# Ternary feed-forward stage: rounded values transposed in fp32, rounding constant removed in ScalarE's copies, silu waiting for the gate product alone

## What is computed

```python
def _weight_quant(w):                       # three matrices, 256 x 1024
    scale = 1.0 / jnp.clip(jnp.mean(jnp.abs(w)), 1e-05)
    return jnp.clip(jnp.round(w * scale), -1.0, 1.0) / scale
def _act_quant(x):                          # per token
    scale = 127.0 / jnp.clip(jnp.max(jnp.abs(x), axis=-1, keepdims=True), 1e-05)
    return jnp.clip(jnp.round(x * scale), -128.0, 127.0) / scale
def _bitlinear(x, w):
    return jnp.einsum('bsi,oi->bso', _act_quant(x), _weight_quant(w))
gate = jax.nn.silu(_bitlinear(x, w_gate))
up = _bitlinear(x, w_up)
return _bitlinear(gate * up, w_down)        # x = x + tanh(g_ffn[1]) * this
```

## Time and profile before

| | us |
|---|---|
| median of 3 runs | 3035.04 |
| lowest and highest | 3032.43, 3036.76 |
| time of the profiled execution | 3036.45 |
| its span | 3034.7 |
| busy in the span: PE, DVE, ACT, POOL | 2558.5, 1635.7, 1290.4, 1218.0 |
| the stage's part of the span | about 857 to 1099 |

### The profile page before, as it was taken

One profiled execution on the slowest core, in us unless ns is written; L12 is line 12 of the kernel. 1 busy time (PEld: TensorE's weight loads), 2 busy tenths in 40 slices (PEclk: granted clock), 3 DMA queues, 4 the chain that ended last, 5 costly groups with the idle time before them and its releaser, 6 DMA issues. The chain is left out here.

```text
span 3034.7 us, 43762 instructions
## 1 busy us (share of the span) xinstructions
PE 2558.5 (84%) x13250; PEld 1481.8 (49%) x13251; DVE 1635.7 (54%) x3292; ACT 1290.4 (43%) x2566; POOL 1218.0 (40%) x1717
## 2 busy tenths in 40 slices
PE   7997999999936647898888889779957886799997
PEld 4554667666613323334343343345534475466664
DVE  5884656555457844665647556378846534222221
ACT  4663435344335532554545446446641232222221
POOL 3665651344446631111120210036890243566663
PEclk9998999999978877999999999989988965899998
DMA  3001000001000004131221221010003241122222
GB/s 122 5 1 60 0 0 1 1 1 42 1 31 0 0 11 89 38 74 47 48 59 47 52 63 38 1 49 15 8 1 111 85 141 54 35 46 45 45 45 31
DMA packets 86053, 117.22 MB, mean 39 GB/s; under 512 B 13864, under 2 KB 64144, under 8 KB 84080
## 3 DMA queue, kind: packets, MB, share of 16 engines
q1 hardware_dynamic: 68944, 96.01, 11.0%
q0 software_dynamic: 16928, 18.93, 4.0%
HBM read 80.00 MB, written 34.64 MB: 38 GB/s over the span
## 5 line engine op out<-in xcount | busy, mean ns | idle before, releaser
L2986 ACT ACTIVATE L2S_pT<-L2S_t_ps 128x512 f32<-128x512 f32 (+3 forms) x768 | 353.7, 490 | 234.7 <-PE L2S_t_ps L2884 125.7
L3065 DVE TENSOR_REDUCE L2S_mx<-L2S_s_ps 128x1 f32<-128x768 f32 (+7 forms) x384 | 347.1, 951 | 110.0 <-PE L2S_s_ps L2863 106.3
L2881 PE MATMUL L2S_t_ps<-L2S_q,L2S_k 98*128 98x512 bf16 (+3 forms) x768 | 250.7, 340 | 41.1 <-ACT L2S_pT L2986 33.1
L2862 PE MATMUL L2S_s_ps<-L2S_k,L2S_q 96*128 96x512 bf16 (+3 forms) x768 | 207.0, 342 | 44.8 <-DVE L2S_mx L3065 33.8
L3170 POOL DMA_DIRECT2D L2S_q<-L2S_mrow x32 | 17.2, 537 | 430.1 <-DVE L2S_mrow L3073 430.1
L3524 DVE TENSOR_TENSOR L3B_h<-L3B_si,L3B_u_ps 128x512 f32<-128x512 f32 x71 | 48.8, 687 | 237.5 <-PE L3B_u_ps L3467 237.5
L571 POOL TENSOR_TENSOR L_prob<-L_prob,L_rc 128x616 f32<-128x616 f32 x64 | 77.9, 1217 | 234.7 <-DVE L_rc L524 234.7
L2881 PEld LDWEIGHTS L2S_t_ps<-L2S_q,L2S_k 98*128 98x128 bf16 x768 | 75.4, 99 | 191.4 <-ACT L2S_pT L2986 147.6
L3441 POOL DMA_INDIRECT out<-L3B_y,L3F_rows x71 | 114.7, 1616 | 132.8 <-DVE L3B_y L3530 118.3
L2899 PE MATMUL L2S_o_ps<-L2S_pT,L2S_v 128*32 128x512 f32 (+3 forms) x1536 | 166.3, 507 | 0.0
L310 PE MATMUL L_scores<-weights,L_xT 128*128 128x308 f32 x512 | 143.1, 423 | 2.2 <-ACT L_xT L426 1.6
(11 more groups left out here) (496 smaller groups left out, 5997.9 us busy)
## 6 DMA issues: line engine op xcount, KB each, us to landing
qk_parts<-L2S_part SPq DMA_DIRECT2D x96, 128.0 KB, 2.3
L2S_q<-qk_parts SPq DMA_DIRECT2D x32, 192.0 KB, 3.6
L2S_k<-qk_parts SPq DMA_DIRECT2D x32, 192.0 KB, 3.5
L2S_q<-qk_parts SPq DMA_DIRECT2D x32, 128.0 KB, 3.3
L2S_k<-qk_parts SPq DMA_DIRECT2D x32, 128.0 KB, 3.3
self_attended<-L2S_att SPq DMA_DIRECT2D x4, 1024.0 KB, 4.3
L_xn<-self_attended SPq DMA_DIRECT2D x8, 512.0 KB, 3.5
L2F_wgu<-in_L_gu SPq DMA_DIRECT2D x8, 512.0 KB, 8.0
```

The source lines that it names most:

```text
L2862: nc.tensor.matmul(o[:, z * 512 + c:z * 512 + e], lhs, k6[0:KR, q % 2, h, c:e], start=True, stop=(e < end))
L2881: mm = nc.tensor.matmul(o[:, lo:512], k6[:, q % 2, j, kt * P:(kt + 1) * P], q6[:, q % 2, j, c * 512 + lo:(c + 1) * 512], start=True, stop= ...
L2986: nc.scalar.activation(pT[:, st % 2, j, lo:512], t_ps[j % 2][:, lo:512], ACT.Exp, scale=SK).then_inc(s["exp_done"], 1)
L3065: nc.vector.tensor_reduce(dst, src, AX.X, ALU.max).then_inc(s["mx_done"], 1)
```

## The change

Eight edits in `ternary_stage`, nothing elsewhere. DVE's rounding of x ends with fp32 values that still hold ROUND (xq); L1972 is gone, and with it the cut at 127. PE transposes xq and hq themselves, in fp32, with the fp32 identity, to fp32 PSUM; hT_ps takes two banks for that, xT_ps still one, and the weights' sums go to o_ps, so that m_ps is gone. ACT's two copies subtract ROUND as they write bf16. DVE's shift and its phase are gone, and PE's turn_h waits for ACT's quantise. The semaphore gu_full is split: g_full behind the gate product, for silu; u_full behind the up product, for DVE's multiply. The gate product waits for silu of the tile before, the up product for DVE's product of the tile before. ACT's quantise of hq waits for the transposes of two tiles before, which now read that buffer. The bf16 identity is gone.

```diff
-        xT_ps, hT_ps, o_ps = ps("xT_ps", [P, 1024], BF16), ps("hT_ps", [P, INNER], BF16), ps("o_ps", [P, 512])
-        m_ps = ps("m_ps", [P, 512])
-        identb = sb("identb", [P, P], BF16)
+        xT_ps, hT_ps, o_ps = ps("xT_ps", [P, 512]), ps("hT_ps", [P, INNER]), ps("o_ps", [P, 512])
...
-                    mm = nc.tensor.transpose(xT_ps[:, k * P:(k + 1) * P], xqb[:, p, k * P:(k + 1) * P], identb[:])
+                    mm = nc.tensor.transpose(xT_ps[:, k * P:(k + 1) * P], xq[:, p, k * P:(k + 1) * P], chip.ident[:])
...
-                pe.wait_ge(s["h_done"], t + 1)
-                for o, n in ((g_ps, "gate"), (u_ps, "up")):
+                for o, n, full in ((g_ps, "gate", "g_full"), (u_ps, "up", "u_full")):
+                    pe.wait_ge(s[("silu_done", "h_done")[n == "up"]], t + 1)
...
-                mm.then_inc(s["gu_full"], 1)
+                    mm.then_inc(s[full], 1)
...
-                pe.wait_ge(s["hqb_done"], t + 3)
+                pe.wait_ge(s["hq_done"], t + 3)
...
-                    mm = nc.tensor.transpose(hT_ps[:, k * P:(k + 1) * P], hqb[:, p, k * P:(k + 1) * P], identb[:])
+                    mm = nc.tensor.transpose(hT_ps[:, k * P:(k + 1) * P], hq[:, p, k * P:(k + 1) * P], chip.ident[:])
...
-                nc.scalar.activation(xT[:, p, :, :].rearrange("p k t -> p (k t)"), xT_ps[:, 0:D], ACT.Copy).then_inc(s["xT_free"], 1)
+                nc.scalar.activation(xT[:, p, :, :].rearrange("p k t -> p (k t)"), xT_ps[:, 0:D], ACT.Copy, bias=-ROUND).then_inc(s["xT_free"], 1)
...
-                act.wait_ge(s["gu_full"], t + 1)
+                act.wait_ge(s["g_full"], t + 1)
...
-                act.wait_ge(s["hqb_done"], t + 1)
+                act.wait_ge(s["hT_full"], t + 1)
...
-                nc.scalar.activation(hT[:, p, :, :].rearrange("p k t -> p (k t)"), hT_ps[:], ACT.Copy).then_inc(s["hT_free"], 1)
+                nc.scalar.activation(hT[:, p, :, :].rearrange("p k t -> p (k t)"), hT_ps[:], ACT.Copy, bias=-ROUND).then_inc(s["hT_free"], 1)
...
-            link(nc.vector.tensor_copy(identb[:], chip.ident[:]))
...
-                link(nc.vector.tensor_scalar(xq[:, p, :], xn[:, p, :], ix[:, p:p + 1], ROUND, ALU.mult, ALU.add))
-                nc.vector.tensor_scalar(xqb[:, p, :], xq[:, p, :], ROUND + 127.0, -ROUND, ALU.min, ALU.add).then_inc(s["xq_done"], 1)
+                nc.vector.tensor_scalar(xq[:, p, :], xn[:, p, :], ix[:, p:p + 1], ROUND, ALU.mult, ALU.add).then_inc(s["xq_done"], 1)
...
-                dve.wait_ge(s["silu_done"], t + 1)
+                dve.wait_ge(s["silu_done"], t + 2)
+                dve.wait_ge(s["u_full"], t + 1)
...
-            def shift(t, q):
-                p = q % 2
-                dve.wait_ge(s["hq_done"], t + 3)
-                dve.wait_ge(s["hT_full"], t + 1)
-                nc.vector.tensor_scalar(hqb[:, p, :], hq[:, p, :], ROUND + 127.0, -ROUND, ALU.min, ALU.add).then_inc(s["hqb_done"], 1)
...
-            pipelined(dve, [stats, normalise, quantise, multiply, shift, none, none], unroll=4)
+            pipelined(dve, [stats, normalise, quantise, multiply, none, none, none], unroll=4)
```

More of the change, by code:

```diff
@@ L1814, in ternary_stage @@
         stat, mv, ve, rs = sb("stat", [P, 2, 6]), sb("mv", [P, 2, 2]), sb("ve", [P, 2]), sb("rs", [P, 2])
-        xn, xq, xqb, xT = sb("xn", [P, 2, D]), sb("xq", [P, 2, D]), sb("xqb", [P, 2, D], BF16), sb("xT", [P, 2, KD, P], BF16)
+        xn, xq, xT = sb("xn", [P, 2, D]), sb("xq", [P, 2, D]), sb("xT", [P, 2, KD, P], BF16)
         am, ax, ix = sb("am", [P, 2]), sb("ax", [P, 4]), sb("ix", [P, 2])
         gs, us = sb("gs", [P, 4]), sb("us", [P, 4])
-        h, hq, hqb, hT = sb("h", [P, 2, INNER]), sb("hq", [P, 2, INNER]), sb("hqb", [P, 2, INNER], BF16), sb("hT", [P, 2, IK, P], BF16)
+        h, hq, hT = sb("h", [P, 2, INNER]), sb("hq", [P, 2, INNER]), sb("hT", [P, 2, IK, P], BF16)
         ah, ai, s2, ev = sb("ah", [P, 2]), sb("ai", [P, 2]), sb("s2", [P, 2]), sb("ev", [P, 4])
         minus1, res = sb("minus1", [P, 1]), sb("res", [P, 2, D])
-        names = """pre abs_done mean_done tern_done stats_done rstd_done xn_done ix_done xq_done xT_full xT_free gu_full silu_done
-            h_done ah_done s2_done hq_done hqb_done hT_full hT_free o_full o_free x_done dve_step pool_step act_step wmean_done""".split()
+        names = """pre abs_done mean_done tern_done stats_done rstd_done xn_done ix_done xq_done xT_full xT_free g_full u_full silu_done
+            h_done ah_done s2_done hq_done hT_full hT_free o_full o_free x_done dve_step pool_step act_step wmean_done""".split()
         s = {n: sem(n) for n in names}
@@ L1836, in _ @@
             pe.wait_ge(s["abs_done"], 3)
-            nc.tensor.matmul(m_ps[:, 0:3], chip.ones[:], rowsum[:], start=True, stop=True).then_inc(s["mean_done"], 1)
+            nc.tensor.matmul(o_ps[:, 0:3], chip.ones[:], rowsum[:], start=True, stop=True).then_inc(s["mean_done"], 1)
             pe.wait_ge(s["tern_done"], 4)
@@ L1883, in _ @@
             act.sem_inc(s["hq_done"], 2)
+            act.sem_inc(s["silu_done"], 1)
             for n, name in enumerate(order):
@@ L1927, in _ @@
         def _(dve):
-            link = Links(dve, s["dve_step"], [1, 1, 1, 1, 0, 0, 0])
+            link = Links(dve, s["dve_step"], [1, 1, 0, 1, 0, 0, 0])
             link.k = 0
-            link(nc.vector.tensor_copy(identb[:], chip.ident[:]))
             dve.wait_ge(s["mean_done"], 1)
-            link(nc.vector.tensor_scalar(wmean[:], m_ps[:, 0:3], 1.0 / COUNT, 1e-5, ALU.mult, ALU.max))
+            link(nc.vector.tensor_scalar(wmean[:], o_ps[:, 0:3], 1.0 / COUNT, 1e-5, ALU.mult, ALU.max))
             nc.vector.reciprocal(wscale[:], wmean[:]).then_inc(s["wmean_done"], 1)
@@ L1944, in _ @@
             dve.sem_inc(s["h_done"], 1)
-            dve.sem_inc(s["hqb_done"], 2)
             link.start = link.k
@@ L1965, in quantise @@
                 p = q % 2
-                link.enter(2, t)
                 dve.wait_ge(s["ix_done"], t + 3)
                 dve.wait_ge(s["xT_full"], t + 1)
-                link(nc.vector.tensor_scalar(xq[:, p, :], xn[:, p, :], ix[:, p:p + 1], ROUND, ALU.mult, ALU.add))
-                nc.vector.tensor_scalar(xqb[:, p, :], xq[:, p, :], ROUND + 127.0, -ROUND, ALU.min, ALU.add).then_inc(s["xq_done"], 1)
-                link.leave()
+                nc.vector.tensor_scalar(xq[:, p, :], xn[:, p, :], ix[:, p:p + 1], ROUND, ALU.mult, ALU.add).then_inc(s["xq_done"], 1)
             def multiply(t, q):
```

## The result

The changed kernel takes 2986.8 us (median of 4 runs, 2984.7 to 2990.3), the kernel before 3034.0 in the same runs: a ratio of 0.9847, interval 0.9832 to 0.9863. The direction and the mechanism were right; the sum came out too small, and the range was too narrow on the side of a larger gain.

The account below looks back on a forecast made before the run. At full clock the PE-ACT ring and DVE bound together at 5.77 us a tile, 6.37 with clock falls. Saving 2.1 by the third silu and 36.2 after (29*5.15+2.0 against 187.6) gave 38.3 off 3035.0: 2997, range 2988 to 3014.

Parts of the forecast that it names:

- the ring: PE and ACT waiting for each other, gate product through silu to the next gate product: 5.77 us a tile at full clock.
- (1): Silu waits for the gate product alone: 0.86 us leaves the PE-ACT chain, 5.77 to 4.91 us at full clock.
- (2): DVE loses the shift and half the x rounding: 4.4 to 4.6 us a tile, no longer the bound.
- (3): POOL's round falls from 5.36 to 5.10, taken as 5.15 (5.0 to 5.3) us a tile, and becomes the bound.
- rival C: DVE and POOL hinder each other anew: 0.3 to 0.5 us more in POOL's round, 5.55 a tile, 3008 us; 14%.
- (4): Chain over two tiles through DVE, POOL and ACT's quantise: 9.63 us, 4.82 a period; POOL may lag about 0.6.
- Rival E: ACT waits for s2, the DVE and POOL chain being longer: 5.7 us a tile, 3013 us; 4%.
- (5): PE's fp32 transposes cost 0.11 us each, 0.88 instead of 0.45 for eight; hidden with 0.3 to spare.
- (6): ACT's copies that read fp32 and subtract: 0 to 0.1 us more, taken as 0.03.
- (7): PE idles 1.45 us a tile instead of 2.0 to 2.4 and stays at 2.4 GHz, so 0.6 us a tile goes.
- rival B: fp32 transposes don't hold PE's clock; some 15 falls at 1.4 us each, 21 of the 38 us, 3018 us; 12%.
- D: Slower: PE's clock, once down, doesn't come back; 7.3 us a tile, 29 us lost, 3064 us; 3%.

Follow-up runs that it names:

- pool_plus: The changed kernel with one more small product of a 128x1 column on POOL in each tile, its result unread: 2994.8 us, ratio 0.987.
- turn_twice: The changed kernel with the eight transposes of hq run twice over: 3002.5 us, ratio 0.988.
- before_busy: The kernel before with 16 unread transposes of the bf16 identity behind each tile's down product: 3009.0 us, ratio 0.991.
- split_only: The kernel before with silu waiting for the gate product only; bf16 path and DVE's shift kept: 3010.3 us against 3035.1, ratio 0.992.
- fp32_only: The changed kernel with silu back behind the up product, leaving fp32 transposes and the missing shift: 3012.4 us, ratio 0.992.
- pool_less: The changed kernel with the addition of 1e-5 to the variance moved from POOL to DVE: 2989.0 us, ratio 0.985.

## What the prediction had right, and the steps of its sum and range that failed

The mechanism stood: the up half left the ring, the clock stayed up, and POOL set the new period. What failed are the sum's term 29*5.15 = 149.4, which charges every step with the steady pace (147.7 measured), its 2.0 us for half-clock stretches (0.5 at most), and the range, which had no bound for the scatter of the executions.

**(1) Silu without the up half.** Right: 1.93 fell to 1.07 us. The ring came out at 4.83 instead of 4.91, as in the kernel before a plain tile at full clock is 5.69 and not 5.77. I had taken 0.52 from ACT's copy of xT to the next gate product out of the one tile I showed; in other tiles it is 0.44, and 0.52 belongs to the step in which the loop turns.

**(2) DVE** is off the path: its product now waits for silu in 28 tiles, 18.5 us in all.

**(3) POOL's round.** Right in kind; that the size fits is luck, since two errors cancel. POOL follows itself with no wait, and its plain round is 5.01 to 5.05 us, less than my 5.10. But two rounds in every four are 5.2 to 5.3, and the mean of the steady part is 5.14, where I had said 5.15. The longer ones show POOL's small operations stretched:

```profile
941.93 0.58 POOL L2023 TENSOR_TENSOR L1F_ai<-L1F_ah,L1F_minus 128x1 f32<-128x1 f32 x1
...
946.97 0.71 POOL L2023 TENSOR_TENSOR L1F_ai<-L1F_ah,L1F_minus 128x1 f32<-128x1 f32 x1
...
951.90 0.39 POOL L2022 TENSOR_SCALAR L1F_ah<-L1F_ah 128x1 f32<-128x1 f32 x1 [0.20 <-POOL L1F_ah L2020]
```

L2023 takes 0.71 instead of 0.56, L2022 0.39 instead of 0.22. That is rival C at a fifth of its price: some 0.1 us a tile and not 0.4. DVE's normalisation runs at that time (951.83 to 952.21 beside the 0.39), as the shift did before; that it is the cause is read from the overlap; no run here took it away, so it stays open. In pool_plus the phases are shifted. The operation that is L2023 here takes 0.56 or 0.57 throughout there and the one that is L2022 still 0.37 in one tile of four, and so 0.27 us more on POOL cost only 0.21.

**(4) The chain through s2** was given 0.6 us of room. ACT's quantise does wait for POOL, in 10 tiles and 5.9 us in all, 3.9 of them in two tiles at the ends. Rival E did not come.

**(5) fp32 transposes.** Right: 8 in 1.04, 0.11 each, covered, with 0.31 to spare by turn_twice.

**(6) ACT's copies.** 1.00 us; the 0.03 were nothing.

**(7) The clock.** Right, and rival B is out: 1.00 in the steady part, and before_busy shows by itself that transposes hold the clock and that the clock was worth 22 us of the stage. I had taken it as 0.6 a tile, 19 us. D did not come near. The reading by idle time fits these runs only if it is all that PE idles in a tile (1.45 forecast, 1.0 to 1.4 measured). It does not fit for one wait: split_only's clock fell behind 1.24 us. The Trainium skill (TensorE: Matmul & The Clock Gate, Part 4: PE-mode transpose) says that transposes do not bring the full clock and are not counted as busy time in the same way. In these runs they held it: with bf16 transposes added, the clock went from 0.84 to 1.00 (before_busy).

**The sum** failed in its last steps. By terms, as the traces of before and after have them:

| term | forecast | measured |
|---|---|---|
| up to the third silu, from the stage's start | -2.1 | -2.6 (39.12 to 36.53) |
| 29 steps at the pace of the steady part | -38.2 (5.15 each) | -39.85 (187.57 to 147.72, 5.09 each) |
| half-clock stretches while the pipeline fills | +2.0 | within the row above, 0.5 at most |
| behind the last silu | 0 | -0.4 (15.80 to 15.42) |
| stage | -38.3 | -42.8 |
| other stages | 0 | -7.1 in the traces, within their scatter |

Two mis-sized terms carry 3.6 of the 4.5 us of the stage. The 2.0 us of half clock were a guess without a row. The one stretch there is runs from 889.7 to 893.1, to 1.6 us behind the third silu's start; ACT's copy of hT waits 0.46 us for PE in it, and the step is 5.04 us all the same. And 5.15 holds only where POOL has its whole round: in the first tiles there is nothing to add to x yet, and in the last no statistics, and there the ring's 4.83 shows through (steps of 4.83 and 4.87, and 4.83 at the very end). I charged all 29 steps with the steady pace. The other 0.9 us are in the first row and in the one behind the last silu. The latter isn't shown to come of the change: that stretch takes 15.8, 13.8 and 13.8 us in the three traces of before and 15.4 to 15.5 in those of after.

The third failure is of the range. It had bounds for POOL's gap and for the rivals and none for the executions themselves: the other stages scatter over 7 us and the stage of the kernel before over 4, and the low end lay only 9 us under the forecast. My own range of 2992 to 3003 was drawn from one term of the sum. With the stage's 4.5 us alone, the time would have been 2992; what took it below the 2988 is outside the stage, within that scatter.

## What to carry to other kernels

Before pricing a shorter chain, list the round of every engine, small instructions included: here the third in line, an engine with 40% of the span, set the new period. A pipeline's steady pace doesn't hold while it fills and drains, since engines lack some of their phases there; charge those steps by the next bound. And take the scatter of the untouched stages into the range from the start, with several traces or at least the spread of the runs.

## What the runs showed of the hardware that I had not expected

- PE work that is of no use can pay: 0.89 us of transposes a tile brought the granted clock from 0.84 to 1.00 and the stage from 242.5 to 220.3 us (before_busy). One wait of 1.96 us went ahead of each fall in fp32_only, but in split_only a wait of 1.24 us did too, with another of 0.96 in the same tile. In the changed kernel, which idles once a tile for 1.0 to 1.4 us, the clock never fell in the steady part.
- The turn of a hardware loop costs time. With four steps to a turn, pool_less has 4.83+5.04+4.83+5.26 = 19.96 us where four plain steps are 19.3, 0.64 more. In the step with 5.04, ACT's silu comes 1.34 us after its last instruction and not 1.13 (the two rows of pool_less). What an engine does in the turn, no run here shows. Only 0.21 of the 0.64 lie in that step; the other 0.43 are in the step of 5.26, behind the tile in which DVE and POOL collide. With eight steps to a turn the two longer steps come half as often.
- Where operations of DVE and POOL meet in these rows, the later one is stretched. In pool_less DVE's rounding of x starts 0.03 us behind POOL's addition and takes 0.85 us instead of 0.35. In one tile it starts 0.12 ahead and takes 0.34, and the addition takes 0.81 instead of 0.73.
- ACT reads fp32 from PSUM as fast as bf16 (1.00 and 1.01 us for 1024 columns), and subtracts a constant on the way. Transposes in fp32 took twice as long as those in bf16, 0.11 us to 0.056 for a 128x128 block at full clock, as the prediction had read.
